# Two routing blocks moved into the end of attention, and the projection of the next-to-last block behind the last scores

## What is computed

```python
x = L0_attn_a_x
x = x + _L0_attn_a_ref(_layernorm(x), Wq, Wk, Wv, Wo, bo)
x = x + _L0_ffn_ref(_layernorm(x), gate_w, gu_w, dp_w, sh_gate_w, ...)
x = x + _L0_attn_b_ref(_layernorm(x), ...)
x = x + _L0_ffn_ref(_layernorm(x), gate_w, gu_w, dp_w, sh_gate_w, ...)

# in the expert sublayer
logits = x @ gate_w.T
topv, topi = jax.lax.top_k(logits, TOP_K)
rw = jax.nn.softmax(topv)
out = sum over the chosen experts of rw * down(silu(gate(x)) * up(x))
out = out + sigmoid(x @ sh_gate1_w.T) * shared(x)
```

## Time and profile before

| what | value |
|---|---|
| median of 3 runs (lowest, highest) | 2075.54 us (2062.52, 2077.22) |
| the profiled execution | 2075.99 us |
| its span, first to last instruction | 2071.7 us |
| busy: PE, PEld, DVE, ACT, POOL | 1725.0, 1074.5, 1440.4, 1111.0, 678.3 us |
| mean granted TensorE clock | 0.868 |
| handover of layer 0 in the span | 528 to 562 us |
| handover of layer 1 in the span | 1556 to 1589 us |

### The profile page before, as it was taken

The page is one execution under the profiler, slowest core; times in us unless marked ns, Lnnn a source line. Parts: engine busy times, 40 slices in busy tenths (PEclk is TensorE's granted clock), DMA queues, the critical chain, the costliest instruction groups (busy, mean ns, idle before and its releaser), DMA issues.

```text
span 2071.7 us, 36352 instructions
## 1 busy us (share of the span) xinstructions
PE 1725.0 (83%) x12410; PEld 1074.5 (52%) x12410; DVE 1440.4 (70%) x3081; ACT 1111.0 (54%) x1975; POOL 678.3 (33%) x764
## 2 busy tenths in 40 slices
PE   6899999999777777888788999999997777779820
PEld 5445454445655566775334454544446566667710
DVE  5678989885566753786537889898846667348843
ACT  2155757666355665664222557575663566566610
POOL 6000101001266455445660001010012663654466
PEclk9577989899888899999885889898898789999965
DMA  7440303000344555565843203040004445556643
GB/s 231 158 63 2 50 16 55 11 2 7 131 180 140 163 154 159 185 199 186 239 152 74 37 2 62 2 62 1 2 7 178 158 144 162 166 154 200 199 154 116
DMA packets 127906, 225.96 MB, mean 109 GB/s; under 512 B 15364, under 2 KB 91028, under 8 KB 123444
## 3 DMA queue, kind: packets, MB, share of 16 engines
q1 hardware_dynamic: 103152, 156.49, 25.0%
q0 software_dynamic: 24576, 67.14, 12.0%
HBM read 124.20 MB, written 98.84 MB: 108 GB/s over the span
## 4 chain that ended last, share of the span: by engine, by line
PE 63%; DVE 11%; issue 8%; DMA 5%; ACT 4%; POOL 4%; another core or an unknown queue 2%; SPq 1%; ACTq 0%; DVEq 0%; POOLq 0%
PE late_banks L1646 14%; PE late_banks L1604 11%; PE late_banks L1449 10%; PE exp_banks L1466 8%; PE exp_banks L1632 7%; POOL ring_t L1037 3%; PE late_banks L1424 3%; DVE chunk_max_t L2055 3%; PE late_banks L1482 2%; DVE inter_t L1936 2%; DMA ring_t<-expert_rows,rows_of_t 2%; PE late_banks L1610 2%; ACT probs_t L1275 1%; DVE hot_t L1758 1%
## 5 line engine op out<-in xcount | busy, mean ns | idle before, releaser
L1275 ACT ACTIVATE probs_t<-exp_banks 128x1024 f32<-128x1024 f32 (+3 forms) x640 | 538.9, 896 | 331.7 <-PE exp_banks L1632 329.5
L2055 DVE TENSOR_REDUCE chunk_max_t<-late_banks 128x1 f32<-128x512 f32 (+1 forms) x960 | 602.4, 683 | 104.6 <-PE late_banks L1604 84.9
L1117 POOL TENSOR_SCALAR_AFFINE_SELECT probs_t<-probs_t 128x512 f32<-128x512 f32 x128 | 81.2, 635 | 809.7 <-ACT probs_t L1275 809.7
L1646 PE MATMUL late_banks<-probs_t,values_t 128*32 128x512 f32 (+3 forms) x2560 | 323.9, 581 | 10.7 <-POOL probs_t L1117 9.9
L1449 PE MATMUL late_banks<-tokensT_t,fetched_t 128*128 x2048 | 309.5, 298 | 27.2 <-ACT fetched_t L1186 16.3
L1032 POOL DMA_INDIRECT ring_t<-token_rows,index_t x256 | 248.5, 971 | 209.6 <-PE late_banks L1424 144.4
L1936 DVE TENSOR_TENSOR inter_t<-late_banks,silu_t 64x256 f32<-64x256 f32 x512 | 217.6, 425 | 141.4 <-ACT silu_t L1203 105.0
L1037 POOL DMA_INDIRECT ring_t<-expert_rows,rows_of_t x256 | 243.7, 952 | 196.2 <-DVE x_sb_t L1954 130.9
L1449 PEld LDWEIGHTS late_banks<-tokensT_t,fetched_t 128*128 128x128 f32 x2048 | 265.4, 203 | 57.5 <-issue 39.7
L1466 PE MATMUL exp_banks<-fetched_t,inter_t 64*128 64x128 f32 x2048 | 195.4, 312 | 91.0 <-DVE inter_t L1936 49.8
L1604 PE MATMUL late_banks<-contextT_t,Qp_t 50*128 50x512 f32 (+7 forms) x640 | 238.9, 523 | 7.1 <-DVE values_t L2024 2.1
(11 more groups left out here) (225 smaller groups left out, 1907.8 us busy)
## 6 DMA issues: line engine op xcount, KB each, us to landing
expert_rows<-outs_t SPq DMA_DIRECT2D x256, 256.0 KB
weights_t<-in_experts SPq DMA_DIRECT2D x8, 1728.0 KB, 13.8
Qp_t<-q_rows SPq DMA_DIRECT2D x12, 768.0 KB
weights_t<-in_experts SPq DMA_DIRECT2D x4, 2112.0 KB, 10.3
q_rows<-part_hi_t SPq DMA_DIRECT2D x16, 512.0 KB, 6.3
k_rows<-part_hi_t SPq DMA_DIRECT2D x16, 512.0 KB, 6.9
Kp_t<-k_rows SPq DMA_DIRECT2D x8, 768.0 KB
q_rows<-part_lo_t SPq DMA_DIRECT2D x16, 256.0 KB, 6.5
```

Source lines behind the costliest of these rows:

```text
L1275: act.activation(probs[:, e % NP, 2 * p:2 * p + 2, off:QB], exp_banks[sq % 2][:, :, off:QB], ACT.Exp, scale=D ** -0.5).then_inc(exp_done, 1)
L1646: last = pe.matmul(pv_banks[n % NPV][32 * h:32 * h + 32, off:QB], values[:, j, GH * g + h, :], probs[:, e % NP, h, off:QB], start=(j == 0) ...
L2055: op = dve.tensor_reduce(chunk_max[:, b, p, chunk_row(r), chunk_col(b, r, c)], bank[:, 0:n].rearrange("q (p k) -> q p k", p=len(parts)), A ...
```

## The change

1. In the planner, the two projections of block 1 (`project` 2 and 3) become ready only when all scores are in the list.
2. Turns and routers of the first two blocks of the routing (places 0 and 1, blocks 3 and 2) go into attention's last steps: turn 0 ahead of the last context, turn 1 behind it, router 0 behind the turning of the last context, router 1 behind the last projection. ScalarE's copies for them stand behind the last copy of the sums. Places 2 and 3 follow with turn and router each.
3. VectorE takes block 1's statistics behind the last division and normalises it behind the last `contextT`; block 0 is normalised in the experts' opening, behind the first MAX8s.
4. GpSimd does the `rstd` of block 1 at the last `ctx`, behind all masks, then its constants, for which it waits for the last sums only, and then the `rstd` of block 0.

The core of the diff:

```diff
+AHEAD = 2
 def core_plan():
+    HALF_LAST = TPB
         if kind == "project":
+            if g < HALF_LAST and at[2] < len(scores):
+                return None
             return max(bank, contexts_at["turn", 2 * g // TPB]) if ("turn", 2 * g // TPB) in contexts_at else None
...
+        PV = len(e_of) // 2
...
         def experts_pool(pool, f):
-            pool.wait_ge(max_free, (f + 1) * MU)
+            pool.wait_ge(pv_done, (f + 1) * PV)
             pool.memset(tokensT[:, KC * SLOTS:KC * SLOTS + P], 0.0).then_inc(pad_set, 1)
...
+            inverse_std(pool, norm_of["f", f], NB - 1)
...
                 for item in plan:
+                    if item == ("ctx", *BLOCKS[-1]):
+                        inverse_std(pool, norm_of[kind, layer] + 1, 2)
...
-                    elif item[0] == "project" and item[1] % 2:
+                    elif item[0] == "project" and item[1] % 2 and item[1] > TPB:
                         inverse_std(pool, norm_of[kind, layer] + 1, place)
                         place += 1
...
+            def keep_turned(f, place):
+
+                for k in range(KC):
+                    u, b = route_turn[f] + KC * place + k, order_of["f", f][place]
+                    act.wait_ge(product, u + 1)
+                    act.activation(plain_xT[:, k, b * QB:(b + 1) * QB], BANK[u % NBANK], ACT.Copy).then_inc(bank_eased, 1)
...
                         act.activation(sums[:, n % 2, :], pv_banks[n % NPV][:, :], ACT.Copy).then_inc(sums_out, 1)
+                        if (g, b) == BLOCKS[-1]:
+                            for place in range(AHEAD):
+                                keep_turned(layer, place)
...
+        def experts_pe(pe, f, turn, router):
+            for place in range(AHEAD, NB):
+                turn(("f", f), place, route_turn[f] + KC * place, xn_route)
+                router(f, place)
...
                     elif item[0] == "ctx":
                         _, g, b = item
                         n = block_no(layer, g, b)
+                        if (g, b) == BLOCKS[-1]:
+                            turn(("f", layer), 0, route_turn[layer], xn_route)
...
                         last.then_inc(max_product, 1)
+                        if (g, b) == BLOCKS[-1]:
+                            turn(("f", layer), 1, route_turn[layer] + KC, xn_route)
                     elif item[0] == "turn_ctx":
...
+                        if (b, k) == (BLOCKS[-1][1], KC - 1):
+                            router(layer, 0)
...
+                router(layer, 1)
                 pe.wait_ge(max_free, (layer + 1) * MU)
...
             top_experts(0)
+            normalise(("ab"[f], f), BLOCKS[-1][1])
             masks(0)
...
+                        if (g, b) == BLOCKS[-1]:
+                            dve.wait_ge(max_free, layer * MU + mu_of["project", TPB - 1] + 1)
+                            statistics(phase, 1)
...
+                        if (b, k) == (BLOCKS[-1][1], KC - 1):
+                            normalise(phase, 1)
...
                         if i % 2:
                             dve.wait_ge(max_free, mu + 1)
-                            statistics(phase, i // 2)
-                            normalise(phase, i // 2)
+                            if i // 2 != 1:
+                                statistics(phase, i // 2)
+                            if i // 2 > 1:
+                                normalise(phase, i // 2)
```

More of the change, by code:

```diff
@@ L1127, in _, with experts_act @@
                     experts_pool(pool, n)
-        def experts_act(act, f):
-            for i in range(KC * NB):
-                u = route_turn[f] + i
-                b, k = order_of["f", f][i // KC], i % KC
-                act.wait_ge(product, u + 1)
-                act.activation(plain_xT[:, k, b * QB:(b + 1) * QB], BANK[u % NBANK], ACT.Copy).then_inc(bank_eased, 1)
+        def experts_act(act, f, keep_turned):
+            for place in range(AHEAD, NB):
+                keep_turned(f, place)
             act.wait_ge(logits_out, NB * (f + 1))
@@ L1294, in _ @@
                 else:
-                    experts_act(act, n)
-        def experts_pe(pe, f, turn, bank_of):
-            phase = ("f", f)
-            def router(i):
-                b, bank = order_of[phase][i], BANK[i]
-                wait_freed(pe, route_turn[f] + KC * (i + 1) - 1)
-                for t in range(TPB):
-                    for k in range(KC):
-                        cols = slice((b * TPB + t) * P, (b * TPB + t + 1) * P)
-                        last = pe.matmul(bank[:, t * GC:(t + 1) * GC], plain_xT[:, k, cols], g_raw[:, k * GC:(k + 1) * GC],
-                                         start=k == 0, stop=k == KC - 1)
-                last.then_inc(routed, 1)
-            for first in range(0, NB, NB // 2):
-                for place in range(first, first + NB // 2):
-                    turn(phase, place, route_turn[f] + KC * place, xn_route)
-                if first == 0:
-                    pe.wait_ge(g_in, 16 * (f + 1))
-                for i in range(first, first + NB // 2):
-                    router(i)
+                    experts_act(act, n, keep_turned)
+        def experts_pe(pe, f, turn, router):
+            for place in range(AHEAD, NB):
+                turn(("f", f), place, route_turn[f] + KC * place, xn_route)
+                router(f, place)
             pe.wait_ge(map_set, 9 * (f + 1))
@@ L1497, in turn, with router @@
                     last.then_inc(product, 1)
+            def router(f, i):
+                b, bank = order_of["f", f][i], BANK[i]
+                if i == 0:
+                    pe.wait_ge(g_in, 16 * (f + 1))
+                wait_freed(pe, route_turn[f] + KC * (i + 1) - 1)
+                for t in range(TPB):
+                    for k in range(KC):
+                        cols = slice((b * TPB + t) * P, (b * TPB + t + 1) * P)
+                        last = pe.matmul(bank[:, t * GC:(t + 1) * GC], plain_xT[:, k, cols], g_raw[:, k * GC:(k + 1) * GC],
+                                         start=k == 0, stop=k == KC - 1)
+                last.then_inc(routed, 1)
             def project_split(place):
@@ L1679, in _ @@
                 else:
-                    experts_pe(pe, n, turn, bank_of)
+                    experts_pe(pe, n, turn, router)
         def experts_dve(dve, f, statistics, normalise, projection):
```

## The result

The changed kernel takes 2058.98 us (median of 20 runs, 2047.10 to 2067.99), the kernel before beside it 2073.65 us (median of 20). The ratio is 0.9932, 95% interval 0.9913 to 0.9950: some 0.7% faster, 14.7 us (10 to 18 by the interval), where 18.4 was forecast. One run of the kernel before was far slower than the rest (2330.22 us) and is left out of the ratio. The profiled execution took 2058.86 us, its span is 2054.7 us against 2071.7.

What follows compares the result with a forecast made beforehand. PE's instruction order was taken as the bound. Per layer 4.4 us stall, 0.5 context, 2.4 projection, 2.4 routing, less 0.4, gave 9.3, taken as 9.2: 2075.5 - 18.4 = 2057.1 us; 2045 to 2068 held 8 in 10.

Steps and rivals of the forecast that it cites:

- the case held likeliest: Whole kernel: the time ends within 1% of the kernel before, chance 0.65.
- Scores before projection: Attention's end: last scores precede block 1's projection, so the last sums start without the mask wait; gain 4.4 us in layer 0.
- Turns between: Around the last context: turns 0 and 1 lie in PE's waits, costing 0.2 and 0.1 us.
- Queues without slack: ScalarE's copies and VectorE's statistics before the context's turning and first router: all cover each other within 0.3 us.
- Projection of block 0: Last projection: starts 4.9 us earlier, takes 3.1 us instead of 5.46; 0.4 us lost to block 1's slower normalise.
- Rest of the routing: Behind the last projection: remaining turns and routers, 1.9 us per router; last logits at 552.0 us, before 561.31.
- A: Rival: PE's clock is low from about 536 to 543 us, 3.6 us per layer lost, 2064 us; chance 0.22.
- B: Rival: transposes keep PE's clock low until the routing ends, 4.6 us per layer later, 2085 us; chance 0.04.
- C: Rival: the expert stage gives back 3 us per layer as its clock drop falls elsewhere, 2063 us; chance 0.12.
- D: Rival: masks not done before block 1's projection ends, so the stall partly stays; margin 1.9 us; 0.02 including the unforeseen.

Runs made afterwards that it cites:

- e7: The changed kernel with unused identity matmuls filling the three waits ahead of the third router, fourth turn and fourth router; ratio 0.9897 to the kernel before.
- e9: The changed kernel with 32 more transposes ahead of turn 0, their results overwritten; one run, 1985.27 us.
- e6: The changed kernel with GpSimd's rstd of block 1 moved behind its constants; ratio 0.9887 to the kernel before.
- e4: The kernel before with the planner's condition and GpSimd's rstd of block 1 behind the last masks, VectorE's order kept; ratio 0.9971.
- e1: The kernel before with only the planner's condition added (block 1's projections behind all scores); ratio 1.0006.
- e5: The changed kernel without the planner's condition and with block 1's rstd and normalise in their old places; ratio 0.9956 to the kernel before.

## Why the prediction came out as it did

The time fell in the range, 2 us above the forecast, and in the case held likeliest, within 1%. In part that is luck: the kernel before came out 1.9 us lower than in the runs that the forecast started from (2073.65 against 2075.54), and against it the gain is 3.7 us short. By its steps:

1. **Scores before projection: right.** The sums start 3.08 us behind the projection's start (forecast 3.1) without a wait. A size was off: they take 0.86 us, not the 1.5 of the earlier trace rows, which was measured at the low clock; the forecast didn't convert that row as it did the others. 0.6 us too much.
2. **Turns between: right.** Turn 0, the sums' transposes, turn 1 and the context's follow at full clock; the context's turning ends at +7.4 (forecast +8.2).
3. **Queues without slack: right.** VectorE's low parts start at 526.54, +7.7 (forecast +8.8), and PE doesn't wait for them.
4. **Projection of block 0: right.** It starts at +9.07 (forecast +10.3) and takes 3.10 us. The normalise beside the constants takes 3.37 and 3.36 us (forecast 3.0).
5. **Rest of the routing: here a step failed.** The sequence was right: the fourth turn waits for block 0's normalise and starts at +18.69 (forecast +19.6), 0.9 us early. But the fourth router, counted at 1.9 us, took 3.53 and 3.22. The clock was weighed only as far as the projection's end ("the new order has none between 528 and 542"), and so far it was right; the step behind it had itself three waits in a row (two copies of 0.6 and the normalise), and what the clock makes of them was not asked. From the projection's start to the last logits it took 15.0 and 14.7 us instead of 12.9, and these came at +24.09 / +23.75 instead of +23.2. e7 shows the cause and its price: 1.5 us at the logits in layer 0.

**The rivals.** A's mechanism (the clock falls for a while) took place, at another place and later than it was put, behind the projection instead of before it, where it costs less: 1.6 and 1.3 us in the fourth router instead of 3.6. B is refuted: the full clock held through the transposes of four more turns (e9). C took place in both layers of the profiled pair, at 2.5 us ahead of the first gather (0.4 in the pair on other chips); the place named for it (VectorE's long work at the opening) was right, the reason, in what can be read, is VectorE beside GpSimd's adds and not the clock. What is lost further behind is measured, 3.2 and 3.5 us, and not explained; executions differ by as much there. D did not occur, its margin of 1.9 us stands in the trace.

**The sum.** 9.3 us per layer were forecast at the logits. Measured are 8.7 and 9.1 at the logits and 9.5 and 9.6 at the one-hot rows, counted from the projection; from a fixed point it is 0.3 less, since the scores now go ahead of the projection. The handover was thus right within 1 us, in part by luck, since two errors of opposite sign met: the way to the projection of block 0 was 1.2 us shorter than forecast, the way from it to the logits 2.1 and 1.8 longer. The total is 14.7 instead of 18.4. The handover's own shortfall at the one-hot rows is near nothing, so the missing 3.7 us lie behind them, as in C; but the upper end of the interval is 18 us, and how much of it is C and how much is noise is not shown. VectorE's slower normalise agrees with the Trainium skill (GPSIMD Engine Reference, Key points), by which the two engines share SBUF interfaces, with contention when VectorE runs in a 2-port mode or has two SBUF inputs. In which mode the normalise ran no trace shows; the size, 3.37 against 1.39 in e6, is the trace's.

## What to carry to other kernels

A wait on the critical chain often sits in several queues at once: with GpSimd's order mended, VectorE's held the same step (e4), so walk all engines' queues before costing one edit. Take every duration with the clock it was measured at. After the largest stall is gone look for the next chain of short waits, since it can lower the clock by itself (three waits of 0.74 to 0.97 us here). Compare stage by stage from a common mark: here 9.7 of 17.0 us between two profiles lay ahead of anything that was changed.

## What the runs showed that was not expected

- The same kernel takes 2074 us on one chip and 1982 to 1984 on three others, 4.4% less; the ratio of the changed kernel is the same on both (0.9932 and 0.9930). Nearly all of it lies in the two expert stages, from the first gather on: 464.1 and 449.4 us in before against 423.6 and 406.2 in e1, while the start of the first handover (528.5 and 528.0) and the second attention (497.2 and 495.3) are alike. Why stays open.
- The clock fell behind a stretch with waits of only 0.74, 0.97 and 0.74 us between dense work, for 6.8 us; in e6, with waits of 0.74 and 0.24, it fell in one layer and not in the other, and in e5, with the same waits, in neither.
- In a dense, long attention stretch (80 to 120 us), where PE is busy 38.57 of 40 us, the granted clock was anywhere from 0.54 to 0.84 between executions, which moves the first handover by some 10 us. What decides it stays open.
